# An edge stage with its key projections ahead of the edge pairs and its table stores awaited only by the gathers

## What is computed

```python
xn = _layernorm(x)
# messages along the edges
hid = relu((xn[src] + edge_attr) @ W1 + b1)
x1 = xn + segment_sum(hid @ W2 + b2, dst)
# linear attention over all nodes, 8 heads of 32
q, k, v = split(xn @ Wqkv)
q = softmax(q, axis=-1) * 32 ** -0.5      # over a head's features
k = softmax(k, axis=nodes)                # over all nodes
out = layernorm_gamma((q @ (k.T @ v)) @ Wout)
x = x + x1 + out
```

## Time and profile before

| what | value |
|---|---|
| time, median of 3 runs | 1470.97 us (1470.77 to 1478.41) |
| the profiled execution, its own time | 1469.43 us |
| span of the profiled execution | 1467.6 us |
| TensorE matmuls, busy | 1176.8 us, 80% of the span |
| VectorE busy | 741.0 us, 50% |
| GpSimd busy | 599.2 us, 41% |
| ScalarE busy | 454.3 us, 31% |
| 313 gathers, L2326 | 301.1 us busy, and idle before them 193.5 us |
| matmuls of the edge pairs, L2338 | 292.8 us busy, idle before them 26.5 us |
| additions of the edge pairs, L2416 | 107.1 us busy, idle before them 194.0 us |

### The profile page before, as it was taken

How to read it: one execution, slowest core, us unless ns; L and a number is a source line. 1 busy time by engine, 2 the same in 40 slices (tenths; PEclk the granted TensorE clock), 3 DMA queues, 4 the chain that set the end, 5 groups by cost and what they waited for, 6 DMA issues and landing times. The chain is left out here.

```text
span 1467.6 us, 22805 instructions
## 1 busy us (share of the span) xinstructions
PE 1176.8 (80%) x7604; PEld 915.5 (62%) x7604; DVE 741.0 (50%) x2374; ACT 454.3 (31%) x916; POOL 599.2 (41%) x700
## 2 busy tenths in 40 slices
PE   3777789898537886176899999998998779985997
PEld 2677789466326655064677777776776554554886
DVE  5999961478663333743434444443345361134332
ACT  2477750432312221012333333333332233331110
POOL 3366630203416665016566565565666100002442
PEclk9899999999759998598999999999999999996999
DMA  5000000400442222754555555555555018367551
GB/s 121 1 2 2 2 2 2 112 4 1 140 138 78 82 77 63 172 161 141 165 161 167 170 167 169 163 163 157 168 167 176 27 43 269 88 164 222 170 187 52
DMA packets 97275, 165.62 MB, mean 113 GB/s; under 512 B 15505, under 2 KB 59181, under 8 KB 96773
## 3 DMA queue, kind: packets, MB, share of 16 engines
q1 hardware_dynamic: 71669, 90.69, 21.3%
q0 software_dynamic: 25488, 73.39, 16.6%
HBM read 138.40 MB, written 27.63 MB: 113 GB/s over the span
## 5 line engine op out<-in xcount | busy, mean ns | idle before, releaser
L2326 POOL DMA_INDIRECT em_gathered<-edge_table,el_which x313 | 301.1, 962 | 193.5 <-DVE em_hidden L2416 111.5
L2338 PE MATMUL em_projected<-em_w,em_attr 128*128 128x256 f32 x1252 | 292.8, 386 | 26.5 <-DVE em_hidden L2416 14.5
L2338 PEld LDWEIGHTS em_projected<-em_w,em_attr 128*128 128x128 f32 x1252 | 238.7, 193 | 72.9 <-issue 40.6
L2416 DVE TENSOR_TENSOR em_hidden<-em_projected,em_gathered 128x512 f32<-128x512 f32 (+1 forms) x157 | 107.1, 684 | 194.0 <-PE em_projected L2338 119.7
L2438 ACT ACTIVATE em_hidden<-em_hidden 128x512 f32<-128x512 f32 (+1 forms) x157 | 98.5, 627 | 249.7 <-DVE em_hidden L2416 189.8
L434 POOL TENSOR_SCALAR nm_hot_a<-nm_order,ek_places 128x125 bf16<-128x125 int16 x150 | 99.6, 672 | 50.7 <-PE nm_banks L558 47.3
L446 DVE TENSOR_SCALAR nm_hot_key<-nm_key_order,ek_keys 128x100 bf16<-128x100 int16 x500 | 117.3, 261 | 0.0
L2821 PE MATMUL oe_banks<-oe_wd,xn_T 128*128 x432 | 98.1, 381 | 0.0
L2749 POOL DMA_INDIRECT oe_hidden<-oe_table,oo_node x27 | 25.9, 960 | 176.3 <-DMA oe_table<-state 125.9
L445 DVE TENSOR_SCALAR nm_hot_a<-nm_order,ek_places 128x125 bf16<-128x125 int16 x350 | 94.2, 271 | 0.0
L2821 PEld LDWEIGHTS oe_banks<-oe_wd,xn_T 128*128 128x128 f32 x432 | 80.6, 191 | 9.9
(11 more groups left out here) (487 smaller groups left out, 2246.4 us busy)
## 6 DMA issues: line engine op xcount, KB each, us to landing
em_attr<-in_edge_attr_sets SPq DMA_DIRECT2D x156, 256.0 KB
oe_table<-state SPq DMA_DIRECT2D x20, 448.0 KB
oe_wd<-in_ffn_Wd SPq DMA_DIRECT2D x8, 1024.0 KB
em_gathered<-edge_table,el_which POOLq DMA_INDIRECT x313
mx_w<-in_ffn_w SPq DMA_DIRECT2D x16, 256.0 KB
oe_table<-state SPq DMA_DIRECT2D x1, 2248.8 KB
state<-in_x SPq DMA_DIRECT2D x5, 448.0 KB
state<-in_x SPq DMA_DIRECT2D x1, 2240.0 KB
```

Source lines behind the costliest of these rows:

```text
L2326: nc.gpsimd.indirect_dma_start(out=gathered[:, n % GATHERED, :], out_offset=None, in_=table, in_offset=bass.IndirectOffsetOnAxis(ap=lanes. ...
L2338: last = nc.tensor.matmul(projected[:, k % BANKS, n % 2, :], attr[:, k % ATTR_RING, (n % 2 * KB + f) * 128:(n % 2 * KB + f + 1) * 128], w1 ...
L2416: nc.vector.tensor_tensor(pair_slots(k), projected[:, k % BANKS, 0:width, :], gathered[:, at:at + width, :], ALU.add).then_inc(pre_ready, 1)
```

## The change

It does four things. The table rows go into `hidden_sum`, a buffer of the same shape that lives through the edge stage, in place of `nf_rows`. The table stage no longer waits for its stores: their semaphore is handed on, and in the edge stage GpSimd waits for it ahead of the first gather, and ScalarE ahead of its loop over the sets, because it later writes `hidden_sum`. SyncE asks for the five weights and clears the semaphores ahead of the stores. And steps 0 to 9 of the attention run on TensorE ahead of pair 0, with all their halves on VectorE and ScalarE (and both halves of step 10); the steps woven into the sets start at 10 and so come five sets earlier than before.

```diff
+TABLE_PARTS = 5
 def normalise_to_first(...):
-        rows = sb("rows", [P, TILES, DIM])
             def _(sp):
                 for k in range(ATTR_RING):
                     load_attributes(sp, A, attr, attr_loaded, k)
+                others.sync(sp)
+                clear(sp, done)
                 for q in range(PARTS):
                     sp.wait_ge(kept, (q + 1) * SIZE)
                     load_rows(sp, table[...], rows[:, q * SIZE:(q + 1) * SIZE, :], stored)
-                others.sync(sp)
-                clear(sp, done)
-                sp.wait_ge(stored, 32 * PARTS)
 def edge_messages(...):
             def _(pool):
                 nc.gpsimd.iota(order_i[:], ...).then_inc(numbered, 1)
+                pool.wait_ge(table_stored, 32 * TABLE_PARTS)
                 for n in range(BLOCKS):
             def _(pe):
+                for u in range(attention.KEYS):
+                    attention.tensor(pe, u)
                 for s in range(SETS):
                     for k in pairs_of(s):
                         project(k)
                         if k % SET_PAIRS == 1:
-                            attention.tensor(pe, 2 * s)
+                            attention.tensor(pe, attention.KEYS + 2 * s)
...
                     if s < SETS - 1:
-                        attention.tensor(pe, 2 * s + 1)
+                        attention.tensor(pe, attention.KEYS + 2 * s + 1)
             def _(dve):
                 attention.vector_first(dve)
+                for u in range(attention.KEYS + 1):
+                    for h in range(2):
+                        attention.vector(dve, u, h)
...
-                        if s < SETS - 1:
-                            attention.vector(dve, k // 2, k % 2)
+                        if s < SETS - 1 and k >= 2:
+                            attention.vector(dve, attention.KEYS + k // 2, k % 2)
             def _(act):
+                for u in range(attention.KEYS + 1):
+                    for h in range(2):
+                        attention.scalar(act, u, h)
+                act.wait_ge(table_stored, 32 * TABLE_PARTS)
...
-                        if s < SETS - 1:
-                            attention.scalar(act, k // 2, k % 2)
+                        if s < SETS - 1 and k >= 2:
+                            attention.scalar(act, attention.KEYS + k // 2, k % 2)
 def layer1(...):
+            table_stored = p.sem("em_table_stored")
-            normalise_to_first(p, c, A, x, xn, xn_T, w1, b1, attr, attr_loaded, table, w, done)
+            normalise_to_first(p, c, A, x, xn, xn_T, w1, b1, attr, attr_loaded, table, hidden_sum, table_stored, w, done)
-            edge_messages(p, c, A, lanes, w1, attr, attr_loaded, table, hidden_sum, attention)
+            edge_messages(p, c, A, lanes, w1, attr, attr_loaded, table, table_stored, hidden_sum, attention)
```

More of the change, by code:

```diff
@@ L1937, in load_attributes, with normalise_to_first @@
     sp.dma_start(attr[:, k % ATTR_RING, 0:2 * DIM if s < SETS - 1 else DIM], source).then_inc(attr_loaded[k % ATTR_RING], 16)
-def normalise_to_first(p, c, A, x, xn, xn_T, w, b, attr, attr_loaded, table, others, done):
+def normalise_to_first(p, c, A, x, xn, xn_T, w, b, attr, attr_loaded, table, rows, stored, others, done):
     nc = p.nc
-    BANKS, PARTS = 4, 5
+    BANKS, PARTS = 4, TABLE_PARTS
     SIZE = TILES // PARTS
@@ L1954, in normalise_to_first @@
         var_ready, std_ready, normed, transposed = sem("var_ready"), sem("std_ready"), sem("normed"), sem("transposed")
-        copied, ready, kept, stored = sem("copied"), sem("ready"), sem("kept"), sem("stored")
+        copied, ready, kept = sem("copied"), sem("ready"), sem("kept")
         s = c.stats[:].rearrange("p (t k) -> p k t", k=6)
@@ L2276, in scalar, with edge_messages @@
             nc.scalar.activation(self.std[:], self.var[:], ACT.Sqrt).then_inc(self.std_ready, 1)
-def edge_messages(p, c, A, lanes, w1, attr, attr_loaded, table, hidden_sum, attention):
+def edge_messages(p, c, A, lanes, w1, attr, attr_loaded, table, table_stored, hidden_sum, attention):
     nc = p.nc
```

## The result

| | kernel before | kernel after |
|---|---|---|
| median of 20 runs each | 1472.68 us | 1467.71 us |
| profiled execution, its span | 1469.43, 1467.6 us | 1468.32, 1466.4 us |
| last store request ends | 644.80 us | 648.97 us |
| edge stage, from there to the next stage's first matmul | 522.8 us | 515.9 us |

The ratio is 0.9958, interval 0.9945 to 0.9971: 0.42% faster, where 0.2% slower was forecast. In the two profiled executions the table stage ended 4.2 us later in the kernel after, so the spans differ less than the stages. Of these, 3.1 us were there before the table stage's first matmul (619.83 and 622.96), where nothing was changed. From that matmul to the end of the last store request it is 24.97 and 26.01 us; with SyncE's old order 24.97 to 25.90 us (25.89 in part_keys), with the new one 24.5 to 26.1 us, so asking for the weights ahead of the stores shows no price there.

What follows compares the result with a forecast made beforehand. The edge stage was taken as bound by a loop of gathers and late TensorE signals, 12.75 us a set. 1469.43 + 3.9 - 1.25 = 1472.1 us, with the median 1.5 us above: 1473.6 us, own range 1467 to 1479, overall 1455 to 1485.

Steps and rivals of the forecast that it cites:

- The start: Edge stage's begin: TensorE starts 0.8 us after the last store request, 5.4 us earlier; first gather at 647.6 instead of 651.71.
- Keys: Row of keys ahead of pair 0: late signals stall it after 16 tiles; keys end at 669.6, first addition at 671.4.
- What is given up for it: Front of the edge stage: four pairs no longer done under the first gathers, 3.9 us later (bounds -2.3 to +8.9).
- The other sets: Steps 10 and up: same order, same 12.75 us a set; five attention-free sets at the end save 1.25 us.
- rival C: Sets against gather ring and banks: another rhythm shifts forty sets by 0.25 us each, 1464 or 1484 us; chance 0.10.
- the prediction's own signs of being wrong: Keys without a gap, attention-free sets at 10 to 11 us, or a middle window without 32 or 33 gathers.
- The sum: Whole kernel: 1469.43 + 3.9 - 1.25 = 1472.1 us profiled, 1473.6 us as median, 0.2% slower; chance 0.48.
- A: Key signals on time, attention-free sets at the gathers' pace: 1455 us, or 1462 with half the second term; chance 0.24.
- B: Keys: TensorE stalls on a key eviction, first addition at 677.1, 1479 or 1486 us; chance 0.18 together with D.
- D: Stage start not SyncE's doing: 5.4 us of earlier start lost, ending near B; chance 0.18 together with B.

Runs made afterwards that it cites:

- part_keys: Kernel before with the keys ahead of the first pair, but SyncE's old order and wait kept: ratio 1.0038 to the kernel before.
- part_start_third: Kernel before with only the new SyncE order and the gathers' own wait, keys woven in as before, on the fourth chip: ratio 0.9947.
- after_fifth: Kernel after, unchanged, rerun on the fourth chip, where signals are late: ratio 0.9990 to the kernel before.
- after_fourth: Kernel after, unchanged, on the fourth chip, where signals are late, 1 run: 1476.98 us against 1475.15 for the kernel before.
- before_ring16: Kernel before with sixteen gather buffers instead of twelve, on the fourth chip: ratio 1.0034 to the kernel before.
- spread16_second: Kernel after with the six attention-free sets spread among the others and sixteen gather buffers, on the fourth chip: ratio 1.0024 to the kernel before.
- after_again: Kernel after, unchanged, rerun on a chip with signals on time: ratio 0.9970 to the kernel before.
- before_again: Kernel before, unchanged, profiled on a chip with signals on time, 1 run: 1380.67 us against 1385.67.
- half_project: Kernel after projecting only the first 128 of 256 features of each edge, 1 run: 1352.52 us against 1386.68 for the kernel before.

## Why the prediction was wrong

**The start: right, and by itself a gain.** TensorE started 0.53 us after the last store request (0.8 predicted), the first gather 2.86 us after it (2.8). The prediction made nothing of the start on its own account, since it was costed only together with the keys. part_start_third shows what it is worth where signals are late: 0.53%.

**Keys: the mechanism right, the price nearly.** The row of keys has gaps, as said: in the profile after they begin once the signals have been on time to about 660, 8.3 us after the first gather (9 predicted). The last gap ended 0.9 us before the twelfth gather's end in the first comparison (666.50 and 667.42) and 2.5 us behind it in after_fifth and after_fourth (1.5 to 3.5 predicted). But TensorE's gaps were of 0.3 to 1.7 us, not one of several. The first addition came 24.7 us after the last store request (26.6 predicted, bounds 20.4 to 31.6), in after_fifth and after_fourth 27.5 and 28.9 us. **What is given up for it** was put at 3.9 us and measured 1.5 in the first comparison, and 4.6 and 5.9 us in after_fifth and after_fourth, taken against the same 35.4 us.

**The other sets: this step failed.** It said "in the same order, at the same 12.75 us", and 1.25 us for the sets without attention. The additions that open the sets show both parts. Timelines of the kernel before (sets 6 and 33 and the last addition) and of the kernel after (sets 1 and 28 and the last addition), where the same steps stand five sets earlier:

```profile
745.62 0.69 DVE L2416 TENSOR_TENSOR em_hidden<-em_projected,em_gathered 128x512 f32<-128x512 f32 x1 [2.62 <-PE em_projected L2338]
...
1089.84 0.68 DVE L2416 TENSOR_TENSOR em_hidden<-em_projected,em_gathered 128x512 f32<-128x512 f32 x1
...
1153.62 0.42 DVE L2416 TENSOR_TENSOR em_hidden<-em_projected,em_gathered 128x256 f32<-128x256 f32 x1 [0.16 <-issue]
```
```profile
685.91 0.69 DVE L2421 TENSOR_TENSOR em_hidden<-em_projected,em_gathered 128x512 f32<-128x512 f32 x1 [5.36 <-PE em_projected L2338]
...
1025.93 0.69 DVE L2421 TENSOR_TENSOR em_hidden<-em_projected,em_gathered 128x512 f32<-128x512 f32 x1 [2.57 <-PE em_projected L2338]
...
1150.67 0.42 DVE L2421 TENSOR_TENSOR em_hidden<-em_projected,em_gathered 128x256 f32<-128x256 f32 x1 [0.16 <-issue]
```

| us | sets 1 to 5, keys and the turning of the maximum | 27 sets with the same steps | the last sets, no attention on TensorE |
|---|---|---|---|
| before | 65.4 | 344.2 (12.75 each) | 63.8 (6 sets) |
| after | none | 340.0 (12.59) | 124.7 (11 sets) |
| after_fifth | none | 343.7 (12.73) | 123.7 (11 sets) |
| after_fourth | none | 342.5 (12.69) | 126.0 (11 sets) |

*The exchanged sets* were to save 1.25 us and saved 4.5 us (65.4 + 63.8 - 124.7), in after_fifth and after_fourth 5.5 and 3.2. The five taken away cost 13.1 us each and not 12.75, the five added (124.7 - 63.8)/5 = 12.2 and not 12.5. The last six sets of the kernel before took 10.6 us each by their additions, already in the trace that the prediction was read from. Its 12.5 was the pace of the gathers, which run up to 20 us ahead of the additions there; that lead falls to 9 us by the last addition. *The sets with the same steps* were to save nothing. They saved 4.2 us in the first comparison, and 0.5 (after_fifth) and 1.7 us (after_fourth) in the last groups, where the start alone, with the old keys, has 12.74 and 12.75 us a set. This is rival C's term, which was put at plus or minus 10 us with a chance of 0.10. What made it 12.59 us in one profile and 12.69 to 12.75 in the others stays open. One of the prediction's own signs of being wrong came up with it, 34 gathers in the window 833 to 884, and another nearly, 11.3 us for sets without attention, where 10 to 11 was to tell against it.

**The sum.** The forecast had +2.65 us: 3.9 for the front and -1.25 for the sets. It became +1.5 and -8.6 in the first comparison, and about +5 and -5.5 on the chip of the last groups (against the parts of the kernel before in the first comparison), where the kernel is at 0.9990 of the one before (up to 1.0012) and the forecast was 1.0018. So the sign was lost on terms of a few us each that nearly cancel. The time, 1467.7 us, lies just inside the forecast's own 1467 to 1479; the stage was missed by more, 6.9 us shorter in the profiles where 2.65 us longer was forecast. The range held the time by its width, with 0.7 us to spare.

**The rivals.** A (faster, everything on time) is the truth of the chips with signals on time, though not by its numbers: there TensorE is the bound, the gain of the change is 0.30 and 0.15% on the two where it was timed, and the sets without attention run at the gathers' pace, as A said, which is there a loss, since TensorE could do them in 9.0 us. The Trainium skill, page "SBUF — State Buffer", section "Who interferes with whom", says that TensorE and ScalarE never wait on anyone. It speaks of the ports of SBUF and not of signals, so it could not carry rival A. No run here shows a matmul held up at a port, on any of the four chips; what was late, by up to 20 us while gathers ran on the fourth, were signals, and that section says nothing of those. B (slower, a stall at the key eviction) was seen in small, 22.9 to 27.1 us for the keys, and decided nothing at twelve buffers; at sixteen the keys ended at 30.0 us and the first addition came at 31.8, past the 30.2 us from which it was to decide. C was the truth in direction in the first comparison, and hardly on the fourth chip. D fell at once: the stage did start with SyncE's last request.

**What stays open.** The kernel before was timed but not profiled on the chip of the last two groups, so the parts of its stage there are compared with those of the first comparison. What holds the signals back, and why three chips don't show it, no run tells; before_ring16 and spread16_second show only that the lateness lasts longer with more gathers in one go.

## What to carry to other kernels

Price a change of order by the sets that it exchanges, and take their pace from the times of one repeated instruction: here the sets taken away cost 13.1 us each and those added 12.2 by the times of the additions, while one pace for all, read from counts of gathers in two windows, gave 1.25 us for 4.5. Compare sets that hold the same steps, not those that have the same number. When work is taken out from under a stream of gathers, ask which of the two is slower in the part that is left: on the chips with signals on time, sets emptied of work became slower than TensorE alone at the very end, and spreading them or four more buffers were worth over 6 us on the one where they were tried. And before a version is called best, run it on more than one chip: spread free sets with sixteen buffers gave 0.9914 on one and 1.0024 on another, the start alone 0.9976 and 0.9947.

## What was unexpected of the hardware

- The same program takes 1386 us on three chips and 1475 us on a fourth, with the granted clock much the same (0.939 in after_again, 0.929 in after_fifth). Between the profiles of the first comparison and of before_again the edge stage holds 67 us of the difference (522.8 and 456.1), and 25 us lie ahead of the table stage's first matmul (at 619.83 and 594.38), which was not looked at; what follows the edge stage takes 300.0 and 302.4 us.
- On the slower chip and in the first comparison the signals of finished matmuls are acted on late, by 1.4 to 1.6 us on average and up to 20 us, while gathers run one behind the other, on several engines at once (SyncE and VectorE at 861.14 and 861.20; ScalarE up to 9.8 us late in the keys of spread16_second). They had been on time for some 7 to 10 us after the first gather. Signals of VectorE and ScalarE were not late: a gather that waited for an addition started 0.27 us after its end.
- A gather every 1.25 us (0.95 and 0.30) was the rate on every chip; with half of the edge matmuls left out, sets of eight gathers took 9.9 us (half_project), which is that rate.
